# Another order of the same pieces in a kernel of eight sublayers: weight splits, decay exponentials, routing and recurrence steps moved

## The reference

```python
x = x + ln(L0_attn(ln(x)))   # mamba block, then a mixture of 8 experts (silu(g) * u, top 2)
x = x + ln(L0_ffn(ln(x)))    # mixture of 64 small experts, top 8, and 2 shared ones
x = x + ln(L1_attn(ln(x)))   # RWKV: time mixing, k, v, r products, the recurrence wkv
x = x + ln(L1_ffn(ln(x)))    # product with a ternary weight
x = x + ln(L2_attn(ln(x)))   # 8 heads, rotary positions, causal window of 32
x = x + ln(L2_ffn(ln(x)))    # 8 tile products, one chosen by position
x = x + ln(L3_attn(ln(x)))   # rotated q, k, v, softmax over 256 tokens, Lorentz norm
x = x + ln(L3_ffn(ln(x)))    # shared expert and 8 experts of 512 hidden units, top 2
```

## Time and profile before

| | us |
|---|---|
| median of 3 runs | 1450.84 |
| the profiled execution, whole | 1445.63 |
| its span, first to last instruction | 1443.8 |
| PE busy | 1135.5 (79%) |
| DVE busy | 981.0 (68%) |
| ACT busy | 720.4 (50%) |
| POOL busy | 615.1 (43%) |

### The profile page before, as it was taken

The page is one execution under the profiler, slowest core; times in us unless marked ns, Lnnn a source line. Parts: engine busy times, 40 slices in busy tenths (PEclk is TensorE's granted clock), DMA queues, the critical chain, the costliest instruction groups (busy, mean ns, idle before and its releaser), DMA issues.

```text
span 1443.8 us, 13324 instructions
## 1 busy us (share of the span) xinstructions
PE 1135.5 (79%) x3910; PEld 570.5 (40%) x3922; DVE 981.0 (68%) x2194; ACT 720.4 (50%) x1376; POOL 615.1 (43%) x426
## 2 busy tenths in 40 slices
PE   4225968877887969678787876968997899999797
PEld 1002323333332323333333533535453465556565
DVE  5965787578866887467657797555645545549787
ACT  7506653476437552442524524435563357756564
POOL 1970787148732965122113574453423122224322
PEclk7557979988899979689898999989998999999898
DMA  6000000000000000200001000000000200000000
GB/s 209 0 0 1 0 1 0 1 0 1 0 1 1 1 0 0 101 0 1 0 1 66 1 1 1 1 1 1 1 1 0 66 0 1 8 1 8 0 9 7
DMA packets 11271, 17.76 MB, mean 12 GB/s; under 512 B 1304, under 2 KB 7584, under 8 KB 10688
## 3 DMA queue, kind: packets, MB, share of 16 engines
q1 hardware_dynamic: 11200, 16.93, 3.5%
...
## 4 chain that ended last, share of the span: by engine, by line
PE 39%; DVE 12%; ACT 5%; issue 3%; POOL 2%; POOLq 0%; DVEq 0%; ACTq 0%
PE bankE L1840 6%; PE bankE L1225 3%; PE bankS L1803 2%; PE bankE L1757 2%; PE bankS L1788 2%; PE bankS L1757 2%; PE bankE L1287 2%; PE bankE L620 1%; PE bankS L1760 1%; PE bankE L1246 1%; PE bankE L1760 1%; PE bankS L1730 1%; PE bankE L579 1%; PE bankE L1275 1%; PE bankE L613 1%
## 5 line engine op out<-in xcount | busy, mean ns | idle before, releaser
L732 DVE TENSOR_TENSOR_SCAN hs<-dA,carry,bankS 128x512 f32<-128x512 f32 x128 | 156.7, 1266 | 3.1
L332 POOL TENSOR_TENSOR hc<-hs,cb 128x1024 f32<-128x1024 f32 x56 | 131.8, 2353 | 46.3 <-DVE hs L732 43.4
L307 POOL TENSOR_TENSOR cv<-cv,hc 128x1024 f32<-128x1024 f32 x56 | 132.6, 2368 | 4.4
L1715 ACT ACTIVATE c_h<-bankE,C 128x512 f32<-128x512 f32 x144 | 98.7, 687 | 53.1 <-PE bankE L1840 50.7
L1609 POOL TENSOR_TENSOR c_acc<-c_acc,c_tw 128x512 f32<-128x512 f32 x32 | 45.9, 1434 | 159.6 <-DVE c_tw L1934 159.5
L443 ACT ACTIVATE sg<-bankE,C 128x512 f32<-128x512 f32 x80 | 54.8, 687 | 97.2 <-PE bankE L579 96.9
L724 DVE TENSOR_TENSOR bankS<-dx,bankS 128x1024 f32<-128x1024 f32 x64 | 78.3, 1224 | 6.5 <-PE bankS L508 5.9
L1840 PE MATMUL bankE<-c_fH,c_w1H 128*128 128x512 f32 x144 | 81.3, 565 | 1.1 <-ACT c_h L1715 1.1
L393 ACT ACTIVATE dA<-dl,Aneg 128x512 f32<-128x512 f32 x128 | 80.2, 708 | 0.1
L508 PE MATMUL bankS<-bc,sel 96*128 96x512 bf16 x60 | 28.0, 466 | 59.6 <-DVE hs L732 59.6
L542 PE MATMUL bankE<-h2T,wg 128*128 128x512 f32 x128 | 71.2, 639 | 4.0 <-ACT sg L424 1.9
...
## 6 DMA issues: line engine op xcount, KB each, us to landing
...
wu<-in_up_T SPq DMA_DIRECT2D x1, 1024.0 KB, 10.2
...
```

The lines of the kernel that those rows point to most:

```text
L307: pool.tensor_tensor(cv[:, :, :], cv[:, :, :], (hv if by_vector(i, k) else hc)[:, :, :], ALU.add).then_inc(s["y_acc"], 1)
L332: pool.tensor_tensor(dst[:, :, :], hs[:, k % HS, :, :], cb[:, k % 2, :].unsqueeze(1).to_broadcast([P, HV, G]), ALU.mult).then_inc(s["hc_re ...
L732: V.tensor_tensor_scan(hs[:, k % HS, h, :], dA[:, (HV * k + q) % DA, :], dbx[:, h, :], carry[:, k, h:h + 1], ALU.mult, ALU.add).then_inc(s ...
L1715: act.activation(h[:, n % 3, :], E[k % 2][:, :], ACT.Gelu_apprx_tanh, bias=col("b1_3", k)).then_inc(s["fs_ready"], 1)
```

## The change

Only the table `ORDER` differs. It holds the same pieces, one line less of text (so every later line has a number lower by 1), in another order: of those with a part on PE 72 of 731 are moved, on DVE 74 of 648, on ACT 49 of 653, on POOL 32 of 290. Every engine has as many instructions as before, and ScalarE loads its function tables as often.

```diff
@@ -94,55 +94,54 @@
 ORDER = [(p[0], p[1:].split(".")[0], int(p.split(".")[1])) for p in """
...
-    cR2.0 cR3.0 cU0.0 cy1.0 cU1.0 cU2.0 cU3.0 cU4.0 cW1.0 cU5.0 cU6.0 cV1.0 cU7.0 cU8.0 cX1.0 cU9.0 cU10.0 cQ0.1 cU11.0 cU12.0 cU13.0 cU14.0
...
+    ct5.0 cE6.0 bX4.3 bX5.3 cT6.0 bX6.3 bX7.3 ct6.0 bA4.3 bA2.3 cE7.0 cT7.0 ct7.0 cY1.0 cI1.0 bA13.3 cR0.0 cR1.0 cR2.0 cU0.0 cy1.0 cS6.0
+    cW1.0 cU1.0 cV1.0 cR3.0 cX1.0 cU2.0 cU3.0 cU4.0 cU5.0 cU6.0 cU7.0 cU8.0 cU9.0 cU10.0 cU11.0 cU12.0 cU13.0 cU14.0 cU15.0 cQ0.1 cU16.0
...
```

More of the change, by code:

```diff
@@ new lines @@
+    aA2.1 an0.1 aM2.0 ao0.1 aN1.1 aM3.0 aA3.1 an1.1 ao1.1 aN2.1 an2.1 aM4.0 aM5.0 aM6.0 ao2.1 aN3.1 an3.1 aM7.0 aM8.0 ao3.1 aN4.1 an4.1
+    aM9.0 aM10.0 ao4.1 aN5.1 an5.1 aM11.0 ao5.1 aN6.1 aM12.0 an6.1 aM13.0 ao6.1 aN7.1 an7.1 aM14.0 ao7.1 aM15.0 aL1.0 aA4.1 aA5.1 aA6.1
+    aA7.1 aN8.1 aL3.0 aL4.0 an8.1 ao8.1 aL5.0 aN9.1 an9.1 aR2.0 ao9.1 aU0.0 aU1.0 aN10.1 aU2.0 an10.1 ao10.1 aU3.0 aR5.0 aN11.1 an11.1 aR6.0
+    ao11.1 aN12.1 aU4.0 an12.1 aU5.0 ao12.1 aN13.1 aU6.0 an13.1 aU7.0 ao13.1 aN14.1 aU8.0 an14.1 aU9.0 ao14.1 aN15.1 aU10.0 an15.1 ao15.1
@@ new lines @@
+    bD0.0 bA0.0 bA10.0 bK2.2 bK3.2 bQ0.0 bQ1.0 bQ2.0 bQ3.0 bC0.0 bK13.2 bc0.0 bN0.0 bA0.1 bC1.0 bV0.0 bH0.0 bK4.2 bK14.2 bc1.0 bN1.0 bW0.0
+    bO0.0 bC2.0 bK5.2 bK8.2 bV1.0 bH1.0 bK15.2 bc2.0 bW1.0 bO1.0 bN2.0 bC3.0 bV2.0 bH2.0 bc3.0 cS0.0 bW2.0 bK16.2 bK7.2 bK9.2 bK6.2 bN3.0
+    bO2.0 bV3.0 bH3.0 bK10.2 bW3.0 bA10.1 bO3.0 bK17.2 bK1.3 bQ0.1 bA1.0 bK11.3 bA11.0 bQ1.1 bQ2.1 bA12.0 bA3.0 bK2.3 bX0.0 bX1.0 bX2.0
+    bX3.0 bX4.0 bX5.0 bX6.0 bX7.0 bA4.0 bA2.0 bQ3.1 bK3.3 bC0.1 bA13.0 bc0.1 bA0.2 bN0.1 bC1.1 bV0.1 bH0.1 bc1.1 bK13.3 bN1.1 bW0.1 bO0.1
@@ new lines @@
+    bC2.1 bK4.3 bV1.1 bH1.1 bc2.1 bW1.1 bO1.1 cS1.0 bN2.1 bC3.1 bV2.1 bH2.1 bc3.1 bW2.1 bK14.3 bK5.3 bN3.1 bO2.1 bK8.3 bV3.1 bH3.1 cS2.0
+    bA10.2 bW3.1 bK15.3 bQ0.2 bO3.1 bK16.3 bQ1.2 bA1.1 bA11.1 bK7.3 bK9.3 bK6.3 bQ2.2 bA12.1 bQ3.2 bK10.3 bA3.1 bX0.1 bX1.1 bX2.1 bX3.1
+    bX4.1 bX5.1 bX6.1 bX7.1 bA4.1 bA2.1 bC0.2 bc0.2 bK17.3 bA13.1 bN0.2 bA0.3 bC1.2 bV0.2 bH0.2 bc1.2 bN1.2 bW0.2 bO0.2 bC2.2 bV1.2 bH1.2
+    cS3.0 cS4.0 bc2.2 bW1.2 cI0.0 cQ0.0 bO1.2 bN2.2 bC3.2 bV2.2 bH2.2 bc3.2 cG0.0 bW2.2 bN3.2 cQ1.0 bO2.2 bV3.2 bH3.2 bA10.3 bW3.2 cG1.0
@@ new lines @@
+    bO3.2 bA1.2 bQ0.3 bA11.2 bA12.2 cH0.0 cZ0.0 bA3.2 cZ1.0 cE0.0 cZ2.0 bX0.2 bX1.2 bX2.2 cE1.0 cT0.0 bX3.2 bX4.2 ct0.0 cZ3.0 cE2.0 bX5.2
+    bX6.2 bX7.2 cS5.0 cE3.0 cT1.0 bA4.2 ct1.0 bQ1.3 cT2.0 bQ2.3 bA2.2 ct2.0 bQ3.3 cT3.0 bC0.3 bc0.3 ct3.0 cZ4.0 cY0.0 bA13.2 bN0.3 bC1.3
+    bV0.3 cy0.0 cW0.0 bH0.3 bc1.3 bN1.3 bW0.3 cZ5.0 cE4.0 bO0.3 bC2.3 bV1.3 cV0.0 bH1.3 bc2.3 bW1.3 bO1.3 bN2.3 bC3.3 bV2.3 bH2.3 bc3.3
+    bW2.3 bN3.3 cZ6.0 bO2.3 bV3.3 bH3.3 cT4.0 bW3.3 ct4.0 bO3.3 bA1.3 bA11.3 bA12.3 cZ7.0 cE5.0 cX0.0 cT5.0 bA3.3 bX0.3 bX1.3 bX2.3 bX3.3
```

78 lines of the change are left out of this document (30 added, 48 removed).

## The result

The change makes the kernel slower: 1454.82 us, median of 12 runs (1451.94 to 1459.06), against 1449.7 of 12 runs of the kernel before on the same chip (1446.39 to 1453.3). The ratio is 1.0032, 95% interval 1.0023 to 1.0042, or 4.6 us more. Forecast were 1447.9 and a gain of 2.9. In what follows a difference in us is a ratio less one, times 1450, so that the columns of runs taken at different times can be compared; a ratio is never taken from two profiles.

The account below looks back on a forecast made before the run. No engine is full (TensorE 79%, VectorE 68% busy), so order matters where an engine waits and the others wait with it. Early losses of +6.0 and gains of -8.9 give -2.9: median 1447.9 us, range 1441 to 1457.

Parts of the forecast that it names:

- early terms: Layer one's groups 1 and 2 and the start of layer three: four losses, 1.6 + 1.0 + 2.3 + 1.1 = +6.0 us.
- edits at nothing: Layer one's group 0, pieces between groups, K pieces among group 3's expert blocks, layer four's full 150 us stretch: booked at zero.
- the middle: Attention of group 0, -0.2 us, and tile products of group 0, -0.6 us, with shorter tile products but K3.3 delaying C0.1's maxima.
- End of layer three: TensorE's waits of 3.49 and 3.15 us, for a copy and the routing weights, shrink or get filled: -4.3 us.
- Layer four: Groups 2 and 3: TensorE's waits of 4.82 us for R1.3's rows and 1.07 for POOL's sum shrink: -3.8 us.
- Group 1, M4 behind o1 and N2: Layer one: TensorE idles 1.9 us before o1's row product, some 0.3 comes back: +1.6 us, between 0 and +3.8.
- Group 2, A3 behind M8: Layer one: ScalarE's exponentials block delays a wb copy that POOL's product needs: +1.0 us, between 0 and +5.1.
- Group 2, N10 behind R2: Layer one: N10's product and scans stand between R2 and R5, and L5 comes later: +2.3 us, between 0 and +4.
- Start of layer three: K2.2 moved behind A10.0 puts recurrence operations ahead of Q0.0: +1.1 us, from -1.3 to +4.4.
- Swallowed losses: Rival, chance 0.21: layer one's losses only fill waits at group ends; 0.9 of +6.0 stays, time 1442.8 us.
- The recurrence loses its cover: Rival, chance 0.25: VectorE from 806 to 896, tile products get no shorter; 6.9 us worse, time 1454.8.
- Late waits come back: Rival, chance 0.20: R3.0's or R1.3's wait moves on, half of -8.1 is left; +1.2 us, time 1452.0.

Follow-up runs that it names:

- e15: Changed kernel with before's order of layer one and of layer two's exponentials; the rest and all splits as changed: ratio 0.9960, -5.8 us.
- e3: Kernel before, with the new order only from K2.2 behind A10.0 to W3.3 of layer three's group 3, and the splits of w1: ratio 1.0014, +2.0 us.
- e1: Kernel before, with the new order only from layer three's end (behind W3.3) on, and the splits of w2: 1439.1 us, ratio 0.9941.
- e2: Kernel before, with the new order only in layer one and the recurrence pieces among it, up to K11.2 and L6.3, no splits moved: ratio 1.0103, +14.9 us.
- e9: Kernel before, with the new order only in layer one's groups 0 and 1 and the boundary to group 2: ratio 1.0006, +0.9 us.
- e13: Kernel before, with the new order in all of layer one up to the start of the last expert phase: ratio 1.0060, +8.7 us.
- e5: Kernel before, with only A3 moved ahead of o3, M8 ahead of o3 and n3 ahead of M6 in layer one's group 2: ratio 0.9998.
- e10: Kernel before, with the new order only from layer one's group 2, behind its second routing piece, to the boundary to the last expert phase: ratio 1.0023, +3.3 us.
- e4: The changed kernel run once more, as the measure for its three parts run alone, against the kernel before: ratio 1.0035, +5.1 us.
- e7: As e6, but with U3.1 left ahead of o11 and N12, against the kernel before: ratio 0.9978, a gain of 3.2 us.
- e6: Kernel before, with only group 2's moves from A4.2 to N12.2 in layer one (L4, A7, N10 behind R2 and U1, U3): ratio 0.9991.
- e12: Order of e1 plus, in layer one's group 2, R2 ahead of N10 with A4 to A7 and L4 moved, against before: 1438.79 us, ratio 0.9910.
- e16: As e12, with layer three's weight splits moved too (all 18 splits as in the change), against before: 1438.67 us, ratio 0.9932.
- e8: Kernel before, with only K1.2 behind U19.3, K11.2 behind L6.3 and K2.2 behind A10.0: ratio 0.9998.
- e14: Kernel before, with only layer two's exponentials and preparation in the new order, including K1.2, K11.2 and K2.2: ratio 1.0009, +1.3 us.

## Why the prediction was wrong

**The step that failed.** The forecast was -2.9 and the result +4.6, 7.5 apart. 4.4 of them are the early terms, with the edits at nothing: booked +6.0, measured 10.4 (4.6 + 5.8) in the changed kernel. The other 3.1 are everything else: booked -8.9, measured -5.8 (e15). The late part alone measured -8.6 against -8.1, so these lie in the middle as far as the runs tell: e3 measured +2.0 against +0.3.

**What held: the late terms.** End of layer three, booked -4.3: in e1, where nothing else is changed, the lag falls 4.0 from W3.3 to U5.0 (5.5 in the changed kernel, where a part of it is what the middle gives back). Layer four, booked -3.8: 3.6 in the changed kernel, 5.1 in e1 and 5.2 in e15. The rows foreseen, TensorE in the changed kernel, answering to the earlier trace rows:

```profile
1134.57 1.09 PE L1729 MATMUL bankS<-ident,c_L 128*128 128x128 f32 x4 [1.73 <-DVE c_pT L1919]
...
1151.32 0.60 PE L1821 MATMUL bankE<-ident,c_wt 128*8 128x128 f32 x4 [0.87 <-DVE c_wt L2032]
...
1320.29 0.66 PE L1729 MATMUL bankS<-ident,c_acc 128*128 128x128 f32 x4 [0.35 <-POOL c_acc L1608]
...
1350.94 0.66 PE L1729 MATMUL bankE<-ident,c_xnE 128*128 128x128 f32 x4 [2.41 <-DVE c_xnE L1899]
```

The wait of 3.49 for c_pT is 1.73, that of 3.15 for c_wt 0.87 (I had said under 0.5), 1.07 is 0.35, and 4.82 is 2.41 where I expected 3.4; the term of -2.7 called for 2.1, so the 3.4 didn't fit my own sum. e1 has the first, third and fourth to the hundredth: 1.73, 0.35, 2.41, and no wait for c_wt.

**What fell first: "Edits at nothing", and the terms of group 2.** By the forecast's own steps:

*Group 1, M4 behind o1 and N2, +1.6.* No loss shows: -0.5 in lag from F9.1 to U13.0 in after, e2 and e9, and +0.9 (-0.3 to +2.2) by runs for all of e9. (In e13, with the same order there, the lag grows by 2.2; that is a collision in group 0's routing, below.) The idle time came, but at half the size and filled later. TensorE, changed kernel, answering to the earlier trace rows:

```profile
154.03 1.02 PE L547 MATMUL bankS<-xw,wu 128*128 128x512 f32 x2
155.98 1.10 PE L612 MATMUL bankE<-hh,wd 128*128 128x512 f32 x2 [0.93 <-DVE acc L874]
157.67 0.39 PE L507 MATMUL bankS<-bc,sel 96*128 96x512 bf16 x1 [0.60 <-DVE hs L731]
```

*Pieces around the boundary to group 2, at nothing.* The lag grows by 1.4 between U13.0 and U18.0 in after, e2, e9 and e13 alike. I had let F5 and F7 cancel against L6 and L7 without following either to a row.

*Group 2, A3 behind M8, +1.0.* The wait foreseen came. GpSimd, changed kernel, answering to the earlier trace rows:

```profile
333.88 1.26 POOL L316 TENSOR_TENSOR xw<-h2T,wb 128x512 f32<-128x512 f32 x1 [2.27 <-ACT wb L453]
```

Alone it costs nothing (e5). With its neighbours the lag from M1.1 to L5.1 grows by 1.7 in after, e2 and e13 and 2.4 in e10; 1.1 of that comes at M12 to M13, where M12 now stands behind n6's scans, an edit that my sum had not named.

*Group 2, N10 behind R2, +2.3.* Here most is lost: 3.4 in after and e2, 3.7 in e10 and e13, from L5.1 to o12.2. VectorE and then TensorE in the changed kernel, answering to the earlier trace rows:

```profile
378.12 2.16 DVE L826 TENSOR_TENSOR wt<-ex,lg 128x256 f32<-128x256 f32 x1
380.20 0.17 DVE L828 RECIPROCAL sm<-sm 128x4 f32<-128x4 f32 x1
380.40 2.36 DVE L830 TENSOR_TENSOR wt<-wt,sm 128x256 f32<-128x256 f32 x1
```

```profile
382.81 0.63 PE L568 MATMUL bankE<-ident,wt 128*64 128x128 f32 x4 [3.99 <-DVE wt L830]
...
385.32 0.61 PE L507 MATMUL bankS<-bc,sel 96*128 96x512 bf16 x1 [1.58 <-DVE hs L731]
...
386.15 1.92 PE L578 MATMUL bankE<-fT,g 128*128 128x512 f32 x2
387.86 1.91 PE L622 MATMUL bankE<-sg,g 128*128 128x512 f32 x2
```

The 3.4 of the changed kernel can be split. VectorE's routing step begins 7.15 later than before (MAX8, 376.63 against 369.48), with a lag of 6.18 at L5.1: 1.0 for N10 and L5 together, where I had booked 1.2 and 1.0. The collision takes another 0.85: both operations are stretched, to 2.16 and 2.36, but before they were 1.31 and 2.37, so one and a half of two collisions were there already, and I had looked at neither. TensorE waits 3.99, then 1.58 for the scans, and has two pairs of products at 1.92 where they take 1.02 at full clock: the other 1.6. The granted clock is 0.83 between 370 and 400, where it was 0.95 before. In the nine profiles with R2 ahead of N10 the pair collides in full in after, e2, e4, e10 and e13, all with M's block moved as well, and in e7; in e6, e12 and e16 (M's block as before) it slips through at 0.42 and 0.42, and there the lag falls by 1.1 to 1.2 from L5.1 to o12.2. The edit of e6 and e7 is the same up to R6.1, and it gains 1.1 in the one profile and loses 1.9 in the other.

The level of the clock sorts all nine. VectorE's first operation starts 2.58 us behind TensorE's first products of U0.1 in each. Where these take 1.12 to 1.18 us, GpSimd begins 0.41 to 0.47 ahead of it and the pair collides; where they take 2.07 or 2.08, GpSimd begins 0.68 or 0.69 behind it and the pair slips through. The same holds for group 0's routing in the five profiles with the new order there: in after, e2, e4 and e9 the products of U0.0 take 2.08 and nothing collides, in e13 they take 1.12 and the pair takes 2.16 and 2.36. So the order decides that the two engines meet within 0.7 us, and the clock's phase decides who is first. My sum had a term for neither.

The profiled execution of e7 was, at 1450.34, the slowest of its 11 runs (median 1448.16), so most of them may have missed the collision. The 12 runs of e6 lie in two clusters, seven from 1446.11 to 1449.07 and five from 1452.27 to 1453.50. That is what a collision that comes and goes would give; with one profile of e6, a fast run that missed it, it isn't shown.

*Start of layer three, +1.1.* From U19.3 to Q3.0 the changed kernel and e8 lose 1.4 in lag, while kernels with before's order there gain 1.3 on before's profile. By runs e8, the term alone, measures -0.3 (-1.5 to +1.0), and e14, with the pieces among M and U, +1.3 (-0.3 to +2.9). The profiles show a loss at this place, the runs don't confirm it.

**The middle, booked -0.8 (+0.3 with K2.2, as e3 has it), measured +2.0 (0.6 to 3.6).** In group 0 and its tile products the sum came out near what was booked: from Q3.0 to Q1.2 the lag falls by 0.3, by 0.2 in e15. That is luck, for the two terms in it missed by about 2 in opposite directions. Up to Q2.1, the attention of group 0, the lag falls by 2.1 (2.7 in e15) where -0.2 was booked. From there to Q1.2, the tile products and what follows, it grows by 1.8 (2.5 in e15) where -0.6 was booked. The pairs of 3.04 us did get shorter. GpSimd, changed kernel, answering to the earlier trace rows:

```profile
870.81 3.08 POOL L1041 TENSOR_TENSOR b_pr<-b_prh,b_mk 128x512 f32<-128x512 f32 x2 [2.02 <-ACT b_prh L1139]
873.85 1.09 POOL L1041 TENSOR_TENSOR b_pT<-b_prh,b_mk 128x512 f32<-128x512 f32 x1
874.90 1.09 POOL L1041 TENSOR_TENSOR b_oaT<-b_prh,b_mk 128x512 f32<-128x512 f32 x1
876.31 2.15 POOL L1041 TENSOR_TENSOR b_pr<-b_prh,b_mk 128x512 f32<-128x512 f32 x2 [0.32 <-PE bankE L1286]
```

The eight operations take 9.59 us where they took 12.71: 3.1 less, 2.2 were booked. TensorE's product at V1.1 (b_pr, L1257 at 902.72) waits for nothing, where it waited 1.64. What I had not looked at is groups 1 to 3 of that layer. Q1.3 moved from ahead of group 2's tile products to behind them. The products come 4.0 earlier for it (the lag goes from 13.8 to 9.8), and Q1.3's operations then stand between them and what follows, which puts the lag at 14.8 by C0.3. TensorE's two longest waits between 1020 and 1070, changed kernel:

```profile
1044.41 0.66 PE L1151 MATMUL bankS<-ident,b_prh 128*128 128x128 f32 x4 [1.06 <-ACT b_prh L1142]
...
1061.09 0.70 PE L1239 MATMUL bankE<-b_mask,b_identb 128*128 128x480 bf16 x3 [1.04 <-POOL b_kTt L1024]
```

Before has neither there; b_kTt is made by the rotation that Q1.3 delays. From Q1.2 to W3.3 that makes +2.6 in after and +4.2 in e15, with part of it given back by U5.0.

**The rivals.** "Swallowed losses" is the opposite of what happened. "The recurrence loses its cover" had the right sign in the wrong place: group 0's tile products did get shorter, and C0.1's maxima start 0.5 later against the first of them (22.8 against 22.3), not 3. Its time of 1454.8 is the measured median only by luck: three of the four losses that it adds up didn't come (the products got shorter, the wait of 1.64 went, the splits' departure was a gain). "Late waits come back" is refuted by e1. The bound that I had set myself, that no group of layer one differs by over 4 us from its term, was kept: group 2 lost 5.1 to 6.0 against 3.3. The bound was too wide to help: the sign came from a sum of errors that were each smaller.

**The base.** The forecast priced edits against one execution that was 4 us below its kernel's median. At one of the two places, around 120 us, the clock rose sooner in it; for the other, between U19.2 and M4.3, no cause was worked out. A sum of differences takes such luck for a property of the order.

**What stays open.** Whether layer one's halves add: 4.2 in runs against 8.7 (5.4 to 12.2), though in the profiles group 2 loses 6.0 in e10 and 5.3 in e13. Of the difference of 4.5 the profile of e13 has 2.5 over that of e9 at U13.0, with the collision in group 0's routing that e9's lacks; how many runs of either have it isn't known. Nor is it shown why TensorE's clock had risen ahead of U0.1 in all five profiles with M's block moved: TensorE stands idle there for 1.1 to 1.4 us ahead of those products, where it is 0.6 in the other four.
